# A causal attention loop: late masks as 32x32 matmuls, the state's turn moved behind the output projection and its copy moved to VectorE

## What is computed

```python
q = (x @ Wq.T) ... 16 heads of 8;  k, v, g = x @ Wk.T, x @ Wv.T, x @ Wg.T ... 4 groups of 8
v = v * sigmoid(g);  q, k = rotary(rms_norm(q)), rotary(rms_norm(k));  q = q * q_gain
a1 = causal_attn(q[:4], k[:4], v);  a2 = causal_attn(q[4:], k[4:], v)   # softmax over keys <= query
y = concat([a1 - lam * a2, a1 + lam * a2]) @ Wo.T
x = layernorm(x + y)                                  # called x1 below, turned it is X0
gf = sigmoid(net(mean over tokens of x))
for _ in range(3):
    x = x + (0.1 + range * (0.7 * gf + 0.3 * sigmoid(net4(x)) - 0.5) * 2) * twist(x)
return layernorm(x_in + x)
```

## Time and profile before

| | |
|---|---|
| time, median of 3 runs | 271.57 us (270.48 to 273.31) |
| span of the profiled execution | 268.1 us |
| TensorE busy | 245.2 us, 91% |
| ScalarE busy | 223.8 us, 84% |
| VectorE busy | 195.6 us, 73% |
| GpSimd busy | 85.7 us, 32% |
| exponentials (L928) | 144 of 128x1024, 1.02 to 1.04 us each |

### The profile page before, as it was taken

How to read it: one execution, slowest core, us unless ns; L and a number is a source line. 1 busy time by engine, 2 the same in 40 slices (tenths; PEclk the granted TensorE clock), 3 DMA queues, 4 the chain that set the end, 5 groups by cost and what they waited for, 6 DMA issues and landing times.

```text
span 268.1 us, 9782 instructions
## 1 busy us (share of the span) xinstructions
PE 245.2 (91%) x3663; PEld 129.2 (48%) x3664; DVE 195.6 (73%) x746; ACT 223.8 (84%) x330; POOL 85.7 (32%) x241
## 2 busy tenths in 40 slices
PE   8359999899999999999999999997998999998980
PEld 4143555546556455464564655644553222223880
DVE  1779579597796977978879779652253777999992
ACT  3267989989999999999999999988864987878685
POOL 8740432425325244162342532512011000000473
PEclk9957999999999999999999999999999999999998
DMA  5303362453626517336155352551300346651045
GB/s 131 84 1 60 62 120 61 84 107 93 117 50 145 105 33 157 78 79 139 42 112 106 90 98 53 124 109 20 71 2 18 75 110 154 149 124 39 19 131 167
DMA packets 58217, 23.60 MB, mean 88 GB/s; under 512 B 42928, under 2 KB 56016, under 8 KB 58192
## 3 DMA queue, kind: packets, MB, share of 16 engines
q1 hardware_dynamic: 57904, 23.24, 39.4%
q10 hardware_dynamic: 288, 0.02, 0.1%
HBM read 5.04 MB, written 2.10 MB: 27 GB/s over the span
## 4 chain that ended last, share of the span: by engine, by line
PE 73%; DVE 8%; ACT 6%; DMA 5%; issue 5%; POOL 2%; ACTq 0%; DVEq 0%; POOLq 0%
PE O L630 10%; PE O L617 10%; PE S L750 8%; PE M L419 5%; DMA qk<-parts 5%; PE S L513 5%; PE S L503 4%; PE M L663 4%; PE S L535 3%; PE M L649 3%; PE S L546 2%; PE S L791 2%; PE S L555 2%; PE O L637 2%; PE S L760 2%
## 5 line engine op out<-in xcount | busy, mean ns | idle before, releaser
L928 ACT ACTIVATE probs_late<-S 128x1024 f32<-128x1024 f32 x64 | 63.4, 1029 | 1.1 <-PE S L535 0.8
L928 ACT ACTIVATE probs_past<-S 128x1024 f32<-128x1024 f32 x64 | 62.4, 1040 | 1.9 <-PE S L503 1.8
L617 PE MATMUL O<-probs_past,values 128*32 128x512 f32 x256 | 34.9, 618 | 1.4 <-ACT o_sb L934 0.7
L1554 POOL TENSOR_TENSOR minus_half_sum<-sum_eps,minus_half 128x40 f32<-128x40 f32 x16 | 4.5, 283 | 73.5 <-DVE estimate L1180 69.7
L1300 DVE TENSOR_TENSOR summed<-M,x_res 128x256 f32<-128x256 f32 x15 | 6.4, 425 | 28.7 <-PE M L663 28.7
L630 PE MATMUL O<-probs_late,mixed 128*32 128x128 f32 x512 | 26.4, 279 | 0.0
L630 PE MATMUL O<-probs_late,values 128*32 128x128 f32 x512 | 25.7, 273 | 0.0
L1429 DVE SCALAR_TENSOR_TENSOR cY<-coup,ratio,Y 128x256 f32<-128x256 f32 x48 | 21.0, 480 | 5.6 <-ACT coup L1028 4.7
L750 PE MATMUL S<-X,cn_w 128*128 128x512 f32 x48 | 25.0, 627 | 0.0
L513 PE MATMUL S<-qk 32*128 32x128 bf16 x512 | 19.0, 219 | 0.3 <-ACT probs_late L928 0.2
L513 PEld LDWEIGHTS S<-qk 32*128 32x128 bf16 x512 | 8.1, 92 | 20.7 <-issue 18.6
(11 more groups left out here) (189 smaller groups left out, 571.9 us busy)
## 6 DMA issues: line engine op xcount, KB each, us to landing
Y<-X SPq DMA_DIRECT2D x48, 128.0 KB, 2.4
xT_in<-in_xT SPq DMA_DIRECT2D x16, 128.0 KB, 2.6
x_res<-in_x SPq DMA_DIRECT2D x16, 128.0 KB, 2.1
out<-result SPq DMA_DIRECT2D x16, 128.0 KB, 1.9
future_in<-in_future SPq DMA_DIRECT2D x1, 256.0 KB, 3.0
qk<-parts SPq DMA_TRANSPOSE x15, 4.9
w_o<-in_w_o SPq DMA_DIRECT2D x2, 64.0 KB, 2.5
cn_w<-in_cn_w SPq DMA_DIRECT2D x2, 64.0 KB, 2.1
```

The lines of the kernel that those rows point to most:

```text
L617: mm = pe.matmul(O[32 * g:32 * g + 32, :], values[p][:, 0, g, s, at:at + 32], probs_past[:, s, g, :], start=m == 0, stop=False)
L928: act.activation(dst, S[TILE_BUFFER[n]][:, :, :], ACT.Exp).then_inc(exp_done[n], 1)
```

## The change

- **Masks.** The 64x64 masks of a late pair become 24 of 32x32, a 32x32 triangle each: 16 for the tiles' own keys (`own_triangles`) and, after the 32x32 scores, 8 for those (`first_triangles`). The score groups come first, one after the other. The middle half's two masks of 64x128 become four of 32x64. One table of masks, `band16`, serves all of them.
- **State.** `turn_x1` of a batch is issued straight behind the next batch's output projection, into the other half of bank M (`X1_HALF`), in place of its slot between the late pairs, one batch step later than before. VectorE copies it (`keep_x1`, now a `tensor_copy`), behind the residual add, which waits for the transposes as well; `sum_x1` follows the roped queries instead of `heads`. TensorE writes out four batches ahead of its loop in place of two.
- **Projection's copy.** On ScalarE, `copy_projection` stands ahead of exponential 3 in place of behind it.

```diff
@@ tensor: late_pair
                 for m in (n, n + 1):
                     late_quarter(p, m, 0)
                 for m in (n, n + 1):
+                    late_quarter(p, m, 1)
+                for m in (n, n + 1):
+                    own_triangles(m)
+                for m in (n, n + 1):
                     first_quarter(p, m)
                 for m in (n, n + 1):
-                    late_quarter(p, m, 1)
-                for m in (n, n + 1):
-                    late_mask(m)
+                    first_triangles(m)
@@ tensor: masks
+            def triangle(n, j, t, e, quadrant):
...
+                return pe.matmul(S[TILE_BUFFER[n]][group_rows(quadrant), j, at:at + 128], band16[group_rows(g), QUARTER:2 * QUARTER],
+                                 unit, start=False, stop=True, skip_group_check=True)
+            def own_triangles(n):
+                for j in range(2):
+                    for t in range(T):
+                        triangle(n, j, t, 1, 0 if t else 3)
+                        triangle(n, j, t, 0, 1 if t else 2)
+            def first_triangles(n):
+                for j in range(2):
+                    for t in range(T):
+                        mm = triangle(n, j, t, 0, 0 if t else 3)
                 mm.then_inc(scores_done[n], 1)
@@ tensor: project
                 reach(pe, n_["summed_done"], b - 3)
+                reach(pe, n_["X0_ready"], b - 4)
@@ tensor: attend
                 if not first and not second:
                     output_projection(b - 2)
+                    if not third:
+                        turn_x1(b - 3)
...
-                if not first and not second:
-                    turn_x1(b - 2, project_more)
@@ scalar: attend
                 exponentials(b, 2)
-                exponentials(b, 3)
                 if project_more:
                     copy_projection(b + 2, p)
+                exponentials(b, 3)
                 exponentials(b, 4)
-                if not first and not second:
-                    keep_x1(b - 2)
@@ vector: add_residual, keep_x1, attend
                 dve.wait_ge(n_["projected"], b + 1)
+                reach(dve, n_["x1_turned"], b)
...
+            def keep_x1(b):
+                at = b * SEQ
+                dve.wait_ge(n_["x1_turned"], b + 1)
+                dve.tensor_copy(X0[:, bass.ds(at, SEQ)], X1_HALF).then_inc(n_["X0_ready"], 1)
...
-                if not first and not second:
-                    sum_x1(b - 2)
...
                 if not first:
                     add_residual(b - 1, 1 - p, half_b - (1 - p))
+                if not first and not second:
+                    keep_x1(b - 2)
                 if project_more:
                     normalize_queries(b + 2)
+                if not first and not second:
+                    sum_x1(b - 2)
                 if not first:
                     output_moments(b - 1)
```

More of the change, by code:

```diff
@@ L303, in block_kernel, with batches @@
         block = ctx.enter_context(nc.Block())
-        def batches(eng, step):
-            step(0, 0, 0)
-            step(1, 1, 0)
-            with eng.Fori(1, BATCH // 2 - 1) as i:
+        def batches(eng, step, apart=1):
+            for n in range(2 * apart):
+                step(n, n % 2, n // 2)
+            with eng.Fori(apart, BATCH // 2 - 1) as i:
                 step(eng.snap(i * 2), 0, i)
@@ L519, in first_quarter @@
                 _, s, h = TILES[n]
-                for t in range(T):
-                    of = 1 - t
-                    keys = slice(96, 128) if of == 1 else slice(0, 32)
-                    for j in range(2):
+                for j in range(2):
+                    for t in range(T):
+                        of = 1 - t
+                        keys = slice(96, 128) if of == 1 else slice(0, 32)
                         rows = group_rows(2 * h + j)
@@ L644, in turn_outputs @@
                 pe.wait_ge(n_["o_ready"], b + 1)
-                reach(pe, n_["X0_ready"], b if not isinstance(b, int) or b < BATCH - 1 else b - 1)
                 if project_more:
                     pe.wait_ge(n_["qkvg_ready"], b + 4)
+                elif bank is M:
+                    pe.wait_ge(n_["summed_done"], b)
+                    pe.wait_ge(n_["X0_ready"], b - 1)
                 for r in range(R):
@@ L677, in attend @@
             def attend(b, p, half_b, general):
-                first, second, last = (isinstance(b, int) and b == n for n in (0, 1, BATCH - 1))
+                first, second, third, last = (isinstance(b, int) and b == n for n in (0, 1, 2, BATCH - 1))
                 project_more = not last and not (isinstance(b, int) and b == BATCH - 2)
@@ L941, in attend @@
             def attend(b, p, half_b):
-                first, second, last = (isinstance(b, int) and b == n for n in (0, 1, BATCH - 1))
+                first, last = (isinstance(b, int) and b == n for n in (0, BATCH - 1))
                 project_more = not last and not (isinstance(b, int) and b == BATCH - 2)
@@ L1641, in constants @@
     triangle = np.triu(np.full((QUARTER, QUARTER), FUTURE, np.float32), 1)
-    edges = masks[:, 256:256 + 2 * EDGE].reshape(2, 2, QUARTER, T, 2, QUARTER)
-    for e, t, at in ((0, 0, 0), (0, 0, 1), (1, 0, 1), (0, 1, 0), (1, 1, 0), (0, 1, 1)):
-        edges[:, e, :, t, at, :] = triangle
-    middle = masks[:, 256 + 2 * EDGE:].reshape(2, 2, QUARTER, 4, QUARTER)
-    middle[:, 0, :, 1:3, :] = triangle[:, None, :]
+    masks[:, 256 + QUARTER:256 + 2 * QUARTER] = np.tile(triangle, (4, 1))
     place = np.arange(128) // QUARTER
```

47 lines of the change are left out of this document (23 added, 24 removed).

## The result

The changed kernel takes **284.31 us** (median of 4 runs, 283.55 to 287.18) against 271.32 us: ratio 1.047, interval 1.042 to 1.053. It is slower, as forecast, but by 13.0 us instead of 6.2, and 0.3 us beyond the range of 270 to 284. The profiled execution is the slowest of the four: 287.18 us, a span of 285.4 (the others 281.7 to 283.2). A run's time is 1.8 us more than its span.

The account below looks back on a forecast made before the run. It took TensorE's work (10.88 us a period) as the bound, then VectorE's loop (11.45). Eleven intervals +6.2, late landing +0.9, last batches -0.9: span 274.3, plus 3.5 gives 277.8 us; range 275.5 to 282.5, with rivals 270 to 284.

Parts of the forecast that it names:

- VectorE's stretch: VectorE's unbroken work from residual add to the end of `heads`: 8.63 us, growing by copy 0.34 and sum 0.33 to 9.30.
- its chain: From the end of `heads` through transposes, copy and output projection to VectorE's next add: 2.26 us before, 2.15 forecast.
- The first rival: VectorE's additions vanish in its idle time and ScalarE sets the period, 10.07: some 261 us, chance 0.13.
- One sign: In the changed profile, ScalarE idle over 1 us a batch, most of it ahead of the last exponential.
- A late pair: TensorE's scores and masks for a late pair of tiles: 0.98 us before, 0.64 forecast, 1.18 at the high end.
- The second rival: No change: small matmuls cost their high end (TensorE 11.1) or VectorE's additions only half; 269 to 274 us, chance 0.12.
- The hand-over: From the end of `heads` on VectorE to TensorE taking it up: forecast 0.06 us, bounds 0.06 and today's 0.27.
- Spare 0.34: Time between the DMA transposes landing, 9.74 us after the add, and TensorE wanting them for past scores, at 10.08.
- I keep two such landings: Transposes by DMA landing late (up to 6.6 us) and making TensorE wait: two, as in the trace before.
- the third rival: Slower still: transposes land late more often, three to six times at 1.4 us each; 282 to 286 us, chance 0.12.
- the first batches 0: At the start, the add at 52.33 follows the first late landing, which a faster TensorE meets all the same: 0.
- The last batches: At the end, without projection, VectorE is light and TensorE's gain shows once: -0.9 us.

Follow-up runs that it names:

- experiment 3: Changed kernel with the sum of X0 moved back into VectorE's wait ahead of the residual add, VectorE's batches 2 and 3 written out: 281.73 us, ratio 1.041.
- experiment 6: experiment 3 with the copy of the turned state given back to ScalarE behind exponential 0, ScalarE's and VectorE's batches written out as TensorE's: 280.53 us, ratio 1.033.
- experiment 1: Kernel before with only the new masks and the new order of the late pairs: 271.04 us, ratio 0.999.
- experiment 2: Kernel before with the state and projection-copy parts of the change and four written-out TensorE batches, but the old masks: 282.82 us, ratio 1.042.
- experiment 9: Changed kernel with an unused 256 KB load issued by SyncE just ahead of the transposes of batches 9 to 12: 292.31 us, ratio 1.075.
- experiment 5: Changed kernel with VectorE's order alone altered, the split ahead of the sum and moments, so that the DMA transposes are issued sooner: 286.56 us, ratio 1.057.
- experiment 10: experiment 5 with the same four unused loads as experiment 9: 286.41 us.
- experiment 7: experiment 1 with VectorE's sines' products and `rotated` of b+2 moved behind `heads` of b-1: 268.80 us, ratio 0.987.

## Why the prediction was right and wrong

**Right: which loop sets the period, and its length.** VectorE's stretch from add to `heads`, forecast 9.30, is 9.23; its chain, forecast 2.15 (0.06+1.03+1.06), is 2.22 (0.05+1.04+1.13); together 11.45 and 11.45. That the sum agrees to 0.01 is luck, since the two errors of 0.07 cancel; the loop is right. The copy, forecast 0.34, and the sum, 0.33, measured 0.33 each. Experiments 3 and 6 take them out one after the other, and the period follows: 11.45, 11.18, 10.84. The first rival (idle time of VectorE absorbs the additions) is refuted by experiment 3: the sum is only free in the wait itself. One sign was wrong in its place: ScalarE idles 1.50 us a batch, but ahead of its copy to `headsT`, and not of its last exponential, which follows that copy.

**Right: the masks and the slack.** A late pair was put at 0.64 and is 0.65; a middle half at 0.34 and is 0.34. The second rival (small matmuls at their high end) falls with them: groups of 32x32 matmuls start 0.05 to 0.07 behind one another (134.86, 134.93, 134.98). The hand-over had 0.2 of slack as read: it went from 0.27 to 0.05 in experiment 1. That the period fell by 0.19 there is luck, 0.33 from the chain less 0.13 that the stretch grew and the forecast did not have.

**Right: what a late landing costs.** Spare 0.34 forecast, 0.3 measured; 1.4 us for a landing of 6.6 forecast. Measured: issue 4.79 after the add (133.83), landing 6.6, add 1.46 to 1.5 behind it, 12.9 in all, which is 1.4 more than 11.45. Experiment 2 has it directly, at a granted clock of 1.00: an interval of 12.95 with a landing of 6.66, 1.4 above its period.

**Wrong: "I keep two such landings".** There were six in the changed kernel, which is the third rival, given 0.12 and 282 to 286 us. I counted the late landings of the trace before as if they belonged to the program, and did not ask what lay beside them. They lie beside packets of instruction loading, which last until the loop's first pass is over, and the change writes out two batches more of TensorE's code: the prediction names that ("TensorE's code before its loop is longer by two batches") and then gives it no price. In the kernel before three such packets (40.5, 54.7, 62.2) fell between transposes; in the changed one five of the first six landed late beside one. So the two that I kept were a matter of timing in one trace. Experiment 1, with no batch more written out, has four late at the start; experiment 9, with the same code as the changed kernel up to its loads, has four of the first six. The step that failed is to take the count of late landings from the kernel before: six in place of two. Experiments 5 and 10 show that lateness is a large part of what the entry and exit pay: with the transposes issued sooner the entry costs 1.4 to 1.9 us above its periods instead of 4.9 to 7.2.

**Wrong: "the first batches 0".** They cost 1.6 to the first add, where the first landing is 6.6 us instead of 5.0 and the clock stands at 0.50 from 29.8 to 33.0 (what each is worth there isn't settled), and 6.4 in the five intervals. By the price found above (what the landing exceeds the spare time by) the lateness in the three full ones (landings of 6.1, 6.5 and 6.6) makes 0.9, 1.3 and 1.4, 3.6 in all. The rest, some 2.7, is the clock, but for 0.1 in the first interval: 0.93 where the add follows its scores by 2.39 instead of 1.46, again 0.94, and 0.68 in 93.99 to 106.12 (12.13), which has no late landing and a clock of 0.84.

**Wrong in size: the clock.** I named a fall to 1.2 GHz as what would refute me, but as all or nothing ("well over 15 us" for a batch). It came in stretches of 3 to 7 us, at 0.7 to 0.9 us for an interval (1.4 once, in experiment 10). The last batches, put at -0.9, were +1.1: the two last intervals are 11.21 and 8.27 against 10.43 and 7.99. In the first of them the clock stood at 0.50 from 199.98 to 203.6, in the work behind a wait of 2.90 for a late landing; in experiment 5, with no such fall, it is 9.86. The other has a granted clock of 1.00 and is 8.27 in experiment 2 as well, but 8.05 with the sum moved (experiment 3) and 7.93 with the copy gone too (experiment 6): its 0.28 goes with VectorE's two additions, which the forecast took to be free there, since VectorE is light.

**The offset.** I added 3.5 us to go from a span to the median, which is 1.8 for each run of the changed kernel (1.9 to 3.6 for the kernel before), plus what the median happened to lie above the profiled run. Of the 11.1 us missed in the span, 1.7 went back through this, and 2.9 since the profiled run was the slowest: 6.5 us between 277.8 and 284.31.

**What stays open.** That instruction packets delay the transposes is shown as a coincidence in 70 of 70 late landings, and by experiment 9 for a load of another kind; no run removed the packets themselves. Nor is it settled why the clock fell behind one wait and not behind its like: in experiment 9 waits of 1.03 and 0.87 us left it up, 1.12 and 0.82 did not. The first add of experiment 6 comes 4.1 us late, and no run says why.

## What to carry to other kernels

Where an engine looks idle for a fifth of each turn, follow the wait back: if it ends in that engine's own earlier result, the idle time is part of a loop, and every instruction put outside it lengthens the turn, while one put inside is free; the order in which the engine does its work (experiment 7) is then worth more than shorter work on the busiest engine. The steady period is only half of the story of a short loop. Of the 15 intervals here five stand at the entry, where instructions are loaded beside the kernel's own DMAs. A transfer with only a few tenths of a microsecond to spare should be priced there at its longest landing, with the clock's answer to the wait on top, and a count of late landings from one trace is no property of the program.

## What the hardware showed that I had not expected

- The transposes by DMA of one batch (with the 128 KB load of the next inputs 0.79 MB in 2736 packets) land after 4.9 us, or after 5.5 to 6.9 with one or two 16 KB packets of instructions in their time, though such a packet is 0.9% of the engines' time. In 60 of the 70 cases the landing follows the start of the last such packet by 2.0 to 2.2 us.
- TensorE was granted 1.2 GHz for 3.3 us behind idle times of 1.0 and 1.3 us close together, though it was busy 11.00 of the 13.72 us of that interval, and for 6.6 us behind idle times of 0.7 and 1.4; behind two equal waits of 1.7 us, in experiments 10 and 5, once it was and once not.
- Score and mask groups of 32x32 follow one another in 0.05 to 0.07 us at 134.86 to 134.98, 16, 8 and 8 matmuls, though the first one's 16 are busy for 0.28.
